# Fourth layer of a graph network: two of sixteen sender tiles made on chip in place of three

## What is computed

```python
h = jnp.maximum(_layernorm(x), 0.0)
e = jnp.concatenate([h[src], h[dst], edge_attr], axis=-1)       # 53125 x 192
m = jax.nn.relu(jax.nn.relu(e @ msg_W1 + msg_b1) @ msg_W2 + msg_b2)
agg = jax.ops.segment_sum(m, dst, num_segments=3125)
y = jax.nn.relu(jnp.concatenate([h, agg], -1) @ node_W1 + node_b1) @ node_W2 + node_b2
x = x + h + layernorm_scaled(y)
```

## Time and profile before

| | us |
|---|---|
| three timed runs | 1441.05, 1428.87, 1434.13 (median 1434.13) |
| the profiled execution | 1446.93, of which the span 1445.1 |
| mean granted TensorE clock of the profiled execution | 0.861 |

### The profile page before, as it was taken

One profiled execution on the slowest core, in us unless ns is written; L12 is line 12 of the kernel. 1 busy time (PEld: TensorE's weight loads), 2 busy tenths in 40 slices (PEclk: granted clock), 3 DMA queues, 4 the chain that ended last, 5 costly groups with the idle time before them and its releaser, 6 DMA issues.

```text
span 1445.1 us, 26860 instructions
## 1 busy us (share of the span) xinstructions
PE 1156.5 (80%) x6976; PEld 773.1 (53%) x6976; DVE 837.8 (58%) x2693; ACT 376.6 (26%) x786; POOL 614.8 (43%) x767
## 2 busy tenths in 40 slices
PE   3888879978778877878673878888888888898994
PEld 2556645535655555557253555556565555565663
DVE  7999985478655555554546444444444544453547
ACT  2677741113212111111012222222122222222221
POOL 4444310004556656560003455555555555555530
PEclk9999989998989898787785888797988887888797
DMA  2000040001111111114203544444444444443430
GB/s 51 0 0 0 0 200 1 0 1 39 19 19 20 21 20 20 19 22 137 65 13 92 146 99 96 97 96 95 97 95 98 99 100 89 99 101 88 97 70 23
DMA packets 142402, 88.37 MB, mean 61 GB/s; under 512 B 98573, under 2 KB 120650, under 8 KB 142234
## 3 DMA queue, kind: packets, MB, share of 16 engines
q1 hardware_dynamic: 124024, 70.28, 18.3%
q0 software_dynamic: 16960, 17.40, 6.9%
q10 hardware_dynamic: 1378, 0.22, 0.1%
HBM read 75.48 MB, written 12.35 MB: 61 GB/s over the span
## 4 chain that ended last, share of the span: by engine, by line
PE 49%; DVE 18%; another core or an unknown queue 14%; issue 11%; DVEq 3%; ACT 3%; DMA 1%; ACTq 1%; SPq 0%
PE seg L1441 9%; PE seg L1482 6%; PE big L1471 5%; PE seg L1562 5%; PE big L1587 4%; PE big L1390 4%; PE seg L1595 4%; PE big L1577 2%; PE seg L1605 2%; ACT A L1223 2%; DVE A L1701 1%; PE seg L1492 1%; DVEq L932 1%; DVE acc_mem L1815 1%
## 5 line engine op out<-in xcount | busy, mean ns | idle before, releaser
L1118 POOL DMA_INDIRECT A<-table,idx x338 | 333.8, 988 | 299.3 <-ACT idx L1199 182.1
L1118 POOL DMA_INDIRECT pair<-table,idx x192 | 192.0, 1000 | 265.8 <-issue 197.5
L1327 ACT COPY A<-big 128x512 f32<-128x512 f32 x104 | 60.9, 586 | 415.2 <-remote 233.9
L1482 PE MATMUL seg<-A,cur 128*64 128x160 f32 x700 | 122.5, 317 | 47.2 <-issue 44.9
L1595 PEld LDWEIGHTS seg<-A 128*128 128x128 f32 x832 | 127.9, 219 | 49.9 <-issue 45.4
L1390 PE MATMUL big<-acc_mem 128*128 128x500 f16 x416 | 121.7, 405 | 25.8 <-DVE acc_mem L1815 12.3
L1562 PE MATMUL seg<-A 128*128 128x384 f16 (+1 forms) x624 | 140.1, 376 | 0.0
L1482 PEld LDWEIGHTS seg<-A,cur 128*64 128x64 f32 x700 | 94.7, 143 | 79.8 <-issue 77.5
L1223 ACT CAST A<-big 128x500 f32 x208 | 125.3, 603 | 46.2 <-PE big L1393 24.0
L1587 PE MATMUL big<-A 128*128 128x512 f32 x208 | 130.1, 713 | 4.9 <-DMA A<-pr_table 2.6
L1266 ACT COPY A<-big 128x500 f32<-128x500 f32 x112 | 62.4, 578 | 261.9 <-remote 127.7
(11 more groups left out here) (240 smaller groups left out, 1581.9 us busy)
## 6 DMA issues: line engine op xcount, KB each, us to landing
A<-drel_flat SPq DMA_DIRECT2D x104, 252.0 KB
A<-in_edge_attr_dram SPq DMA_DIRECT2D x103, 128.0 KB
spilled_adjacency<-A SPq DMA_DIRECT2D x1, 7074.0 KB, 18.3
A<-spilled_adjacency SPq DMA_DIRECT2D x6, 1152.0 KB, 11.7
A<-table,idx POOLq DMA_INDIRECT x338
A<-in_src_dram SPq DMA_DIRECT2D x78, 64.0 KB
A<-pr_table SPq DMA_DIRECT2D x104, 31.5 KB
pair<-table,idx POOLq DMA_INDIRECT x192
```

The source lines that it names most:

```text
L1118: pool.indirect_dma_start(out=rows[:, q, j, 0:D], out_offset=None, in_=table, in_offset=bass.IndirectOffsetOnAxis(ap=idx[:, q, j:j + 1], a ...
L1482: op = nc.tensor.matmul(seg[0:D, 2 + buf, 0:SC], cur[:, s, :], stage1[:, buf, s, :], start=(s == 0), stop=(s == NC - 1))
```

## The change

```diff
-MADE = (1, 2, 3)
+MADE = (1, 3)
 NM = len(MADE)
```

## The result

The kernel after takes 1458.72 us (median of four runs, 1457.93 to 1459.88), the kernel before, run beside it, 1437.59 us. The ratio is 1.0156 with a 95% interval of 1.012 to 1.0193: 21 us slower. The forecast was 1465 us.

What follows compares the result with a forecast made beforehand. The fourth layer's loop was taken as paced by runs of gathers, their landing, three ACT instructions and POOL's start. Terms 31.5 + 3.9 - 3.2 - 1.8 = +30.4 us on the 1434.1 us median gave 1465 us, range 1436 to 1484.

Steps and rivals of the forecast that it cites:

- PE paces: Rival, fourth layer's loop: PE sets the time, every made tile less gives back 1.78 us, -46 us, 1388 us; chance 0.04.
- POOL's gathers and waits adding up to the whole stretch: Step, 850 to 1350 us: gathers 270.2, issue waits 86.2 and index waits 144.2 us make 500.6 us, the whole stretch.
- Nothing moves until 1048.40: Step: in the 3.66 us pause after the gather ending at 1046.85, nothing moves until ACT copies the transposed rows.
- only when the run of gathers is over: Step: PE's completions reach the other engines only after POOL's run of gathers; DVE's read-out starts 3.9 us late.
- 13 x 1.26 + 7.0 = 23.4: Step: 13 gathers at 1.26 us plus pauses of 3.66 and 3.35 us make the loop's iteration, 23.4 us.
- What would show it: Expected profile: 364 gathers, 52 read-outs, runs of seven, pauses 3.3 to 3.7 us, iteration 24.7 to 25.0, PE some 45 us lighter.
- The signs against it: Prediction wrong if runs exceed eight gathers, pauses fall under 3 us, or PE's completions reach ACT inside a run.
- the forecast -1.8 us: Term, after the last gathers: PE is alone on the chain, group 2's made tile goes there, -1.8 us once.
- The gather, 1.26 us: Term, POOL's run of groups 2 and 3: one more gather costs 1.26 us in 25 iterations, +31.5 us.
- The longer run's pause: Term, pause after groups 2 and 3: 0.31 us more after seven gathers would be 7.8 us; half taken, +3.9 us.
- irregular pauses: Term, POOL's issue waits: surplus partly from a late PE; at most 6.5 us comes back, the middle taken, -3.2 us.
- the rule of the Trainium skill: Step, DVE and POOL: `senders`' seven `tensor_scalar` hinder gathers, so 4.5 us would come back; nothing taken.

Runs made afterwards that it cites:

- e5: Kernel before with ACT's copy of the indices moved ahead of copy_rows and hidden; chip A, 1391.93 us, ratio 0.9774 to before.
- e10: Kernel before plus a fourth gather for group 2 that nothing reads, its third tile still made; chip A, 1449.29 us, ratio 1.0215 to before.
- b_before: Kernel before, unchanged, run for its profile on chip A; 1426.47 us in the profiled run, median of the timed ones 1423.1 us.
- b_after: Kernel after, unchanged, on chip A; 1444.43 us, ratio 1.0134 to before.
- e7: Kernel after with group 2's third tile neither made nor gathered, its sender features left out; chip B, 1183.2 us, ratio 0.9846 to before.
- e8: Kernel before plus a fourth gather for group 2 that nothing reads, its third tile still made; chip B, 1214.59 us, ratio 1.0101 to before.
- e9: Kernel after, unchanged, on chip B; 1213.65 us, ratio 1.0091 to before.
- e3: Kernel after with MADE = (1,): one made tile and 15 gathers an iteration; chip B, 1242.77 us, ratio 1.034 to before.
- e1: Kernel after with group 2's third tile neither made nor gathered, its sender features left out; chip B, 1183.16 us, ratio 0.9837 to before.
- e2: Kernel before plus a fourth gather for group 2 that nothing reads, its third tile still made; chip B, 1213.45 us, ratio 1.0092 to before.
- e4: Kernel after with ACT's copy of the indices moved ahead of copy_rows and hidden; chip B, 1211.79 us, ratio 1.0081 to before.
- e6: Kernel after with POOL waiting after each group's gathers until they have landed; chip A, 1601.51 us, ratio 1.125 to before.

## Why the prediction was right, and where its sum was off

**The bound was read rightly.** The page had PE at 80%, and a 44 us lighter PE made the kernel slower. The chain of a run, its landing, three ACT instructions and POOL's start stands in the profile after as in the one before. e5 moved one link of it, and the time moved by 31 us. e10 added only the gather, and the time rose by 26 to 31 us. "PE paces" (-46 us) falls: for chip A by the result, and on chip B the whole relief without the gather is 19 us. A lower clock isn't what makes the change slower either. In 850 to 1350 us on chip A the granted clock is 0.88 in `b_before` and 0.82 in `b_after`, but e10 loses as much at 0.88.

**Three steps of the working don't hold as written.**

- POOL's gathers and waits adding up to the whole stretch say nothing about POOL: busy and idle time add up to the stretch on every engine. What carries the argument is what ends the pauses.
- "Nothing moves until 1048.40", and completions get through "only when the run of gathers is over", say too much. PE's results of the first part of a run mostly get through at once. Beside the wait for "remote" of the earlier trace rows (191.3 us, 28 times) ACT's copy waited 43 times for PE by name. One such copy starts at 1040.40, inside the run of the earlier trace rows, right behind its transposes. And one of the late signals passes before the landing: DVE's L1673 waited 4.28 us and starts 0.1 us after the end of the last gather (1046.85):

```profile
ACT A L1327 <- PE big L1577: 119.3, 43, 7.0
```

```profile
1039.69 0.60 PE L1577 MATMUL big<-ident,A 128*128 128x128 f32 x4
...
1040.40 0.59 ACT L1327 COPY A<-big 128x512 f32<-128x512 f32 x1 [3.20 <-PE big L1577]
...
1040.52 0.48 DVE L1760 TENSOR_SCALAR A<-A,row_of 126x512 bf16<-126x512 f32 x1
...
1040.74 1.07 POOL L1118 DMA_INDIRECT A<-table,idx  x1 [0.30 <-issue]
...
1046.95 0.33 DVE L1673 TENSOR_TENSOR A<-iota_r,drel 128x168 f32<-128x168 f16 x1 [4.28 <-remote]
```

- 13 x 1.26 + 7.0 = 23.4 comes out by luck. It counts the 0.30 us in front of a gather also at the two pauses, 0.6 us too much, and takes all gathers at 0.96 us where the mean is 0.99, 0.4 us too little.

**What would show it.** 364 gathers and 52 read-outs are there, and both halves have runs of seven. PE has 44 us less work in a span that is 11 us longer, so its idle time grew by 55 us, and L1327 waits for "remote" for 322.6 us. PE's L1562 is down to this from the earlier trace rows, 43 us less:

```profile
776.00:1400.00 624.00, 96.03 (x400) 39.87 (x400) 0.82 0.40 95
```

The iteration is 24.7 us, at the low end of the forecast 24.7 to 25.0. The signs against it were drawn too sharply. Of the 50 pauses after 820 us, 33 are 3.3 to 3.7 us long, 9 are longer and 5 are under 3 us, but 6 of 50 are under 3 us in before too. Three of 50 runs have ten gathers, and one in the loop's start-up has 14. `b_before` has one of ten too, and they are too few to pace the loop. And in after, four copies L1327 still start on time inside a run, as 30 of 84 did in before (850 to 1350 us).

**The sum was +30.4 us, the timed result +21 us, the two profiled executions differ by +11.1 us.** The two profiles split up by POOL's timeline:

| | before | after | difference |
|---|---|---|---|
| begin of the third iteration | 824.29 | 817.68 | -6.6 |
| from there to the last gather's end | 568.4 | 587.9 | +19.5 |
| from there to the end of the span | 52.4 | 50.6 | -1.8 |

The first line doesn't repeat: on chip A (`b_before`, `b_after`) the same point moved by +1.7 us (812.4 and 814.1), and the spans by +25.5, so it isn't counted as the change's. The tail is the forecast -1.8 us and -1.1 us on chip A. But e10, which keeps all made tiles, has a tail 4.3 us shorter than `b_before`, so the tail moves for other reasons as well. The second line is 0.81 us in each of 24 iterations. In `b_after` it is +24.9 us, 1.04 each, and in e10 +27.1 us, 1.13 each, both against `b_before`. The prediction had (31.5 + 3.9 - 3.2) / 25 = 1.29.

The stretch of 850 to 1350 us tells which term was off. POOL's time there is gathers, 0.30 us in front of each gather inside a run, and pauses (all of the rest, whether the profile names ACT's copy of the indices or "issue" at their end). On chip A the gathers' groups of before and after are these:

```profile
L1118 POOL DMA_INDIRECT A<-table,idx x278 | 274.8, 988 | 225.1 <-ACT idx L1199 133.8 <-issue 91.3
```

```profile
L1118 POOL DMA_INDIRECT A<-table,idx x287 | 276.3, 963 | 224.5 <-ACT idx L1199 147.1 <-issue 77.4
```

With the number of waits named issue (233, 240, 237, 242 and 244), this is an iteration in us:

| | before | after | `b_before` | `b_after` | e10 |
|---|---|---|---|---|---|
| gathers | 12.87 | 13.64 | 12.85 | 13.48 | 13.83 |
| 0.30 us inside runs | 3.33 | 3.55 | 3.32 | 3.54 | 3.57 |
| pauses | 7.64 | 7.48 | 7.20 | 7.41 | 7.14 |
| iteration | 23.84 | 24.66 | 23.38 | 24.43 | 24.55 |

- *The gather, 1.26 us.* Alone it costs that: e10 has 0.98 + 0.25 = 1.23 us more than `b_before` in the first two lines. With the relief beside it, it costs 0.77 + 0.22 = 0.99 us in the case and 0.63 + 0.22 = 0.85 us on chip A, because all gathers got shorter, from a mean of 990 to 974 ns and from 988 to 963 ns. That gives back 0.22 to 0.35 us an iteration, 6 to 9 us in all, where the prediction took nothing. This is the term that was mis-sized, in both pairs.
- *The longer run's pause, +0.16 us, and irregular pauses, -0.13 us.* The regular part came in full, where the prediction took half: the median pause is 3.36 us after six gathers in before and 3.63 us after seven in after, 3.27 and 3.57 us on chip A. Against that, pauses of over 4.5 us are gone: five of 50 in before and three of 55 in `b_before`, none in after and `b_after`. All pauses together changed by -0.16 us in the case and +0.21 us on chip A, so the irregular ones fell by 0.4 to 0.5 us and by 0.1 us. In the case that is beyond the bound of 6.5 us in 25 iterations, on chip A it is not. It was put down to a late PE, but e10, with PE's whole work, has none of the long pauses either (-0.06 us in all). What ends them no run here isolates.

The prediction had the shorter gathers as the rule of the Trainium skill (SBUF — State Buffer, Who interferes with whom: a DVE `tensor_scalar` in a two-port mode and a GpSimd instruction exclude each other), priced at 4.5 us. It took nothing, with the argument that only the gather at a run's begin is slow. The trace shows slow ones inside runs too (1040.74 above). They do go with a `tensor_scalar`, but not with those of `senders`: of the 55 gathers over 1.00 us in before, 46 began while L1760 ran (`receivers`, which the change leaves) and 5 while L1739 or L1740 ran. After, 34 are over 1.00 us and 24 of them began in L1760. With the gather alone, and so with `senders` of three tiles still on DVE, the mean stays at 988 ns. On chip B, though, it is 971 with three and 973 with two. So the shorter gathers go with the relief on chip A, and why is not shown.

**What PE's relief is worth on chip A** is the difference of e10 and the kernel after: ratios of 1.0215 (1.0149 to 1.028) and 1.0134 (1.0087 to 1.0181). The medians give 1449.29 - 1423.53 = 25.8 and 1444.43 - 1423.1 = 21.3 us, so some 5 us, and the intervals overlap. The prediction's -3.2 - 1.8 fits in size, but a value of zero isn't excluded: the profiled execution of e10 is even 3 us shorter than that of `b_after`. Relief alone was not run on chip A.

**On chip B the sign is the same for another reason.** Relief alone gives -19 us, gather alone +12 us, and both together +12 us and not -7. With 13 gathers POOL would need 13 x 1.27 = 16.6 us an iteration, and e7's 13 gathers run at that pace: 298 of them fill 290.1 + 90.8 = 380.9 us. Before is 19 us slower than e7, 0.75 us an iteration, so PE would set it there with three made tiles, at 16.6 + 0.75 = 17.35 us. No trace of before on chip B shows it, but e8, with the same work on PE, has PE busy for 391.0 of 400 us (750 to 1150 us), which is 17.4 us an iteration. With 14 gathers POOL needs 17.8 us and sets the pace with three made tiles (e8) as with two (e9). The bound moves over from PE to POOL within this one change, and after that a further gather costs nearly its full length: e3 is 29 us above after, 1.1 us an iteration.

## What to carry to other kernels

The engine with the highest busy share was the wrong one to relieve at the price of work for another. Take the engine that gets the new work, and ask what ends its waits in the loop: if its own run of work stands in that chain, the new work costs its full step. When a tile can be made by either of two engines, price it on both in the same iteration: on one chip relief alone was worth 19 us, and nothing once the other engine had the tile. A wait that the profile calls "remote" in a program of one core deserves a look at what runs beside it. And where the engine that ends the wait does several things in a fixed order, the one that is waited for can go first (e5: 31 us).

## What the runs showed of the hardware

The same kernel took 1202 us on chip B, 1423 us on chip A and 1437 us beside the kernel of the result. The fourth layer's loop takes 24.4 to 24.7 us an iteration in the kernel after on the slower ones and 17.8 us on chip B. It is not the fourth layer alone: in 340 to 570 us POOL issues 138 and 140 gathers in after and `b_after` and 173 in e9.

On the slower ones PE's completions reach ACT late when they fall well into a run of gathers. Late means here that ACT's copy L1327 starts over 1 us after both the modelled end of its transposes (L1577) and the end of ACT's work before. From 850 to 1350 us, of the transposes that ended in a run:

| | in its first 3.5 us | later |
|---|---|---|
| before | 1 of 28 late | 29 of 32 late |
| `b_before` | 2 of 36 | 31 of 32 |
| after | 6 of 9 | 34 of 37 |
| e9, chip B, after 850 us | | 0 of 71 |

The late ones start 3.8 us late on average in before and 4.8 us in after, at most 6.0 and 6.7 us, and nearly all of them 0.8 to 1.8 us after the end of the run's last gather. The 3.5 us are where the count was split, and the earliest late one ended 2.7 us into its run in before. On chip B none is over 0.12 us late, although POOL never pauses.

The granted clock goes with the chip: 0.945 to 0.951 for e1, e2, e4, e7, e8 and e9 and 0.91 for e3 on chip B, 0.85 to 0.89 for `b_before`, `b_after`, e5 and e10 and 0.83 for e6 on chip A, 0.86 for both kernels of the result. Why the chips differ stays open, and so does whether the lower clock is a cause or follows from the waits. It was not tried to hold the signals back on chip B, and e6 did not free them on chip A in a way that would tell.
